# Field-embedding transposes of four tiles in one visit, and a ring of six gathered tiles

## The chip, the cores and the metric

The kernel runs on one core of one Trainium2 chip. The metric is the device time of one execution in microseconds (us); shorter is better. A time given "beside the span" is that of the execution that was profiled; the span runs from the first to the last profiled instruction.

## The reference

The computation is a recommendation tower over 2048 samples. Each sample has 40 id fields, and each id looks up a row of 64 floats in its field's table. All 780 pairs of fields are combined bilinearly, and the pair values go with 16 dense values through a small network:

```python
e = jnp.stack([tbl_0[ids[:, 0]], ..., tbl_39[ids[:, 39]]], axis=1)   # 2048 x 40 x 64
viW = jnp.einsum('bpd,pde->bpe', e[:, i_idx, :], W)                  # 780 pairs i < j, W[p] is 64 x 64
z = jnp.einsum('bpe,bpe->bp', viW, e[:, j_idx, :])                   # 2048 x 780
h = jnp.concatenate([z, dense_ctx], axis=1)
h = jnp.maximum(h @ W_top1 + b_top1, 0.0)    # 796 -> 512
h = jnp.maximum(h @ W_top2 + b_top2, 0.0)    # 512 -> 256
y = h @ W_top3                               # 256 -> 1
```

Everything is float32.

## The kernel before

The 2048 samples are worked in four chunks of 512. Chunk 0 is worked in two halves (called parts, `q` = 0 and 1) of 256 samples. Two neighbouring fields make a tile of 128 columns, so there are 20 tiles.

Per chunk there are N = 196 steps, 784 in all; in this text a step's number counts through all chunks (chunk 1 starts at 196, chunk 2 at 392, chunk 3 at 588). A step multiplies on TensorE (PE) into one of three buffers of `u` (two PSUM banks each), and VectorE (DVE) multiplies the buffer elementwise with the partner fields. There are two kinds. A column step (124 per chunk, PE line L1038, DVE line L952) keeps the samples in the free dimension; its product is summed over the 64 values by PE with a band of ones into `zacc` (L1052), two columns in one sum. A row step (72 per chunk, PE line L1024, DVE line L921) keeps the samples in the partitions; its product is summed by ScalarE (ACT, L838, 16 activations per row step), by DVE (L962) or by GpSimd (POOL, L755). `make_reducers` chooses who.

The fields have to arrive first. POOL issues indirect DMAs (L734), each of 128 rows of 64 floats; a tile of a whole chunk takes eight of them. Tiles 0 to 3 go to `first_fields`, the others to `gathered`, a ring of GRING tiles. Each issue waits for a step of DVE's progress (`issue_step`, from CHUNK_STEPS: first step and steps per field) and, for a ring slot, until PE has transposed what was in it. Two tiles (t, t+1) make one transpose, written (chunk, i, part) below, with t = 2i: PE transposes 128x128 blocks into one `u` buffer (L996), eight for a whole chunk and four for a half, and ACT copies the buffer to `emb` (L799), after two further copies for `emb_swap` (L797) where i = 2.

All engines follow one list, `ORDER`. Before a step come the transposes that are due at it (TRANSPOSE_STEPS, in the order chunk, part, i). At some transposes of the next chunk a group of the top network (`top`, L1084, L1090, L1096, L1103) of the chunk before is put behind them (TOP_STEPS), and twice per chunk the finished row sums are turned (`turn`, L1070, copied by ACT at L817 and L821). The function `make_room` moves ACT's row sums: one that stands less than HOLD = 2 pair steps ahead of a transpose is held back and written behind it. The `u` buffers go round in the order of their uses (pairs, transposes, turns, tops), so a use needs the third use before it to be done: multiplied, or copied by ACT.

I call a stretch of PE's order that holds only transposes, turns and tops a visit. Its instructions use the array in tiles of 128 rows, where the pair and sum steps use tiles of 64 rows by 32 columns.

Of the kernel before, what the change touches and what calls it, by code (L numbers as in the profile page):

```python
# [36 lines left out]
PRING = 6  # L37
LAG = 4
UBUF = 3
GRING = 4  # L40

SLOT = 4
WRING = 7
# [13 lines left out]
TOP_GROUPS = M1 // 2 + M2 // 2 + 1  # L57


TOP_FIRST = 18  # L60
TOP_EVERY = 19
# [7 lines left out]

FIRST_PART = 40  # L70
FIRST_STEPS = 2
CHUNK_STEPS = {1: (115, 3.9), 2: (280, 4.9), 3: (480, 4.9)}

POOL_FROM = 275

# [138 lines left out]
N = len(WHOLE)  # L214
# [21 lines left out]
def parts(c):  # L236
    return range(PARTS) if c == 0 else range(1)
# [8 lines left out]
def blocks_of(c, q):  # L246

    count = SUB // len(parts(c))
    return range(q * count, (q + 1) * count)
# [141 lines left out]
def make_needs():  # L391

    needs = {}
    for c in range(CHUNKS):
        for n, s in enumerate(STEPS[c]):
            for t in tiles_used(s):
                needs.setdefault((c, part_of(c, n), t // 2), n)
    return needs


NEEDS = make_needs()
# [19 lines left out]
def emb_before(c, i):  # L421

    x = c * TSTEPS + i - EMB_RING
    return EMB_LAST[divmod(x, TSTEPS)] if x >= 0 else None
# [7 lines left out]
def issue_step(c, q, f, s):  # L432

    if c == 0 and q == 0:
        return 0
    f += blocks_of(c, q).index(s) / len(blocks_of(c, q))
    i, j = int(f // 4), f % 4
    here = NEEDS[c, q, i]
    before = NEEDS[c, q, i - 1] if i else here - 4
    in_time = c * N + before + j * (here - before) / 4 - 14  # L440
    begin, every = CHUNK_STEPS[c] if c else (FIRST_PART, FIRST_STEPS)
    steady = begin + every * f
    return max(1, int(min(in_time, steady)))
# [7 lines left out]
def make_transpose_steps():  # L451

    out = []
    for c, i, q in TRANSPOSES:
        need = c * N + NEEDS[c, q, i]
        if c == 0 and q == 0:
            at = max(need - TRANSPOSE_LEAD, 0)
        else:
            issued = issue_step(c, q, 4 * i + 3, blocks_of(c, q)[-1])
            at = min(need - TRANSPOSE_LEAD, issued + LANDING[c])  # L460
            if emb_before(c, i) is not None:
                at = max(at, emb_before(c, i) + 2)
            assert issued <= at <= need
        out.append((at, c, i, q))
    return out


TRANSPOSE_STEPS = make_transpose_steps()


def make_top_steps():

    out = []
    for c in range(1, CHUNKS):
        at = [x for x, *_ in TRANSPOSE_STEPS if c * N + TOP_FIRST <= x < (c + 1) * N - TOP_EVERY][:TOP_GROUPS]
        while len(at) < TOP_GROUPS:
            at.append(at[-1] + TOP_EVERY)
        out += at
    return out


TOP_STEPS = make_top_steps()


# [16 lines left out]
def make_gathers():  # L501
# [3 lines left out]
    for c in range(CHUNKS):  # L505
        for q in parts(c):
            for t in range(T):
                place = ("first", t)
                if t >= FT:
                    rings[c, q, t] = len(rings)  # L510
                    place = ("ring", rings[c, q, t] % GRING)
                filled[place] = filled.get(place, 0) + 2 * len(blocks_of(c, q))
# [97 lines left out]
def pair_tower(nc, ids, tables, w_pairs, w_rows, dense, w1, b1, w2, b2, w3, y):  # L610
# [6 lines left out]
    with ctx:  # L617
        def sb(name, shape, dt=f32):
            return ctx.enter_context(nc.sbuf_tensor(name, shape, dt))

        def sem(name):
            return ctx.enter_context(nc.semaphore(name))
# [4 lines left out]
        first_fields = sb("first_fields", [P, 2, SUB, FF * DIM])  # L627
        gathered = sb("gathered", [P, GRING, SUB, P])
        emb = sb("emb", [P, 2 * EMB_RING, CB])
# [30 lines left out]
        first_gathered = [sem(f"first_gathered{t}") for t in range(FT)]  # L660
        rows_gathered = [sem(f"rows_gathered{i}") for i in range(GRING)]
        rows_transposed = sem("rows_transposed")
# [40 lines left out]
        def _(pool):  # L703
# [6 lines left out]
            def gather(c, q, t, e, s):  # L710
# [3 lines left out]
                if first and t < FT:  # L714
# [3 lines left out]
                    if c >= 2:  # L718
                        pool.wait_ge(rows_transposed, TURN_OF[c - 2, t // 2, len(parts(c - 2)) - 1] + 1)
                elif first and RING_USE[c, q, t] >= GRING:  # L720

                    at, part, tile = RING_ORDER[RING_USE[c, q, t] - GRING]
                    pool.wait_ge(rows_transposed, TURN_OF[at, tile // 2, part] + 1)
# [7 lines left out]
                else:  # L731
                    to = gathered[:, RING_USE[c, q, t] % GRING, s, e * DIM:(e + 1) * DIM]
                    done = rows_gathered[RING_USE[c, q, t] % GRING]
# [463 lines left out]
```

## Time and profile before

| | |
|---|---|
| time, median of 3 runs | 1158.18 us (1156.47 to 1160.94) |
| the profiled execution's own time | 1160.57 us |
| its span | 1158.8 us |
| PE busy | 1105.2 us (95%) |
| DVE busy | 947.9 us (82%) |
| ACT busy | 859.5 us (74%) |
| POOL busy | 744.8 us (64%) |
| TensorE's mean granted clock | 0.994 |

Busy is the union of an engine's instruction times. A matmul's end is modelled, so what PE lost at a place is better read from the starts of its instructions than from the idle time shown.

### The profile page before, as it was taken

What the parts mean: (1) busy time and instruction counts of PE and PEld (TensorE: products, weight loads), DVE (VectorE), ACT (ScalarE), POOL (GpSimd) and SP (SyncE); (2) the same over time, 40 slices, a digit from 0 to 9 for tenths busy, and PEclk for the clock granted to TensorE, in tenths of its full rate; (3) what the DMA queues carried; (4) which work ended last, traced back from release to release, by engine and by line L of the source; (5) the groups of instructions that cost most, each with busy time, mean ns of one, the idle gap of its engine ahead of it and who ended that gap; (6) DMA issues with size and microseconds to landing.
All of it is one profiled execution on the core that took longest, in us unless ns stands there. A gap on an engine that the chain in (4) does not pass through costs nothing.

```text
span 1158.8 us, 52361 instructions
## 1 busy us (share of the span) xinstructions
PE 1105.2 (95%) x21232; PEld 506.7 (44%) x21232; DVE 947.9 (82%) x830; ACT 859.5 (74%) x6607; POOL 744.8 (64%) x898
## 2 busy tenths in 40 slices
PE   2699989999999999999999999999999999999998
PEld 1356757665643333333363333333354333333333
DVE  0699878999859689999976689999984968999960
ACT  0677857999958569999965457898982845799971
POOL 7776777777756555778777567788777756522310
PEclk9999999999999999999999999999999999999999
DMA  6344444444423332232322232222222323211000
GB/s 187 83 121 131 125 121 121 130 139 130 103 52 87 86 88 72 76 86 76 77 63 78 71 93 76 76 78 77 77 68 49 94 73 93 70 58 58 19 3 18
DMA packets 60594, 98.02 MB, mean 85 GB/s; under 512 B 17072, under 2 KB 17088, under 8 KB 60352
## 3 DMA queue, kind: packets, MB, share of 16 engines
q1 hardware_dynamic: 35568, 64.57, 18.1%
q0 software_dynamic: 20480, 21.01, 9.3%
q10 hardware_dynamic: 4304, 9.09, 2.4%
q8 instruction: 167, 2.74, 1.0%
q14 instruction: 75, 0.61, 0.2%
HBM read 94.60 MB, written 0.01 MB: 82 GB/s over the span
## 4 chain that ended last, share of the span: by engine, by line
PE 76%; ACT 9%; POOL 5%; issue 5%; DVE 4%; DMA 1%; DVEq 0%; POOLq 0%
PE u L1038 30%; PE u L1024 18%; PE zacc L1052 15%; ACT row_prod L838 8%; PE u L1084 7%; PE u L996 3%; POOL gathered L734 3%; DVE prod L952 2%; PE u L1096 2%; POOL first_fields L734 1%; DVE row_prod L921 1%; POOL row_prod_p L755 1%; DMA gathered<-tbl,index 1%; PE u L1090 1%; PE u L1070 0%
## 5 line engine op out<-in xcount | busy, mean ns | idle before, releaser
L838 ACT ACTIVATE row_prod<-row_prod 128x64 f32<-128x64 f32 x3248 | 776.5, 242 | 65.9 <-DVE row_prod L921 65.7
L952 DVE TENSOR_TENSOR prod<-u,emb 128x1024 f32<-128x1024 f32 x496 | 588.8, 1217 | 102.0 <-PE u L1038 100.4
L734 POOL DMA_INDIRECT gathered<-tbl,index x512 | 484.7, 947 | 221.9 <-issue 121.5
L838 ACT ACTIVATION_READ_ACCUMULATOR row_prod<-row_prod 128x1 f32 x3248 | 613.1, 189 | 0.0
L1038 PE MATMUL u<-emb,weights 64*32 64x512 f32 (+1 forms) x9760 | 523.1, 507 | 3.5 <-DVE prod L952 2.1
L1024 PE MATMUL u<-row_weights,emb 64*32 64x512 f32 (+5 forms) x5632 | 337.7, 522 | 7.1 <-ACT emb L799 2.3
L1038 PEld LDWEIGHTS u<-emb,weights 64*32 64x32 f32 x9760 | 200.9, 107 | 235.7 <-issue 114.4
L921 DVE TENSOR_TENSOR row_prod<-u,first_fields 128x1024 f32<-128x1024 f32 x203 | 246.9, 1216 | 62.1 <-PE u L1024 61.8
L1052 PE MATMUL zacc<-prod,band 64*32 64x512 f32 (+1 forms) x4960 | 277.1, 504 | 0.7 <-DVE prod L952 0.5
L755 POOL TENSOR_TENSOR row_prod_p<-row_prod_p 128x512 f32<-128x512 f32 (+4 forms) x210 | 128.8, 614 | 90.8 <-DVE row_prod_p L921 77.1
L1024 PEld LDWEIGHTS u<-row_weights,emb 64*32 64x32 f32 x5632 | 118.4, 109 | 147.4 <-issue 56.7
L1052 PEld LDWEIGHTS zacc<-prod,band 64*32 64x32 f32 x4960 | 106.4, 107 | 115.4 <-issue 104.0
L734 POOL DMA_INDIRECT first_fields<-tbl,index x128 | 121.4, 948 | 49.9 <-issue 26.5
L799 ACT ACTIVATE emb<-u 128x1024 f32<-128x1024 f32 (+1 forms) x50 | 42.4, 849 | 86.5 <-PE u L996 86.3
L1084 PE MATMUL u<-z,w12s 128*128 128x512 f32 x192 | 85.6, 603 | 0.0
L853 ACT ACTIVATE h<-u,b1s 128x512 f32<-128x512 f32 x16 | 10.1, 684 | 80.6 <-PE u L1090 80.6
L1084 PEld LDWEIGHTS u<-z,w12s 128*128 128x128 f32 x192 | 36.4, 193 | 44.1 <-issue 43.7
L921 DVE TENSOR_TENSOR row_prod_p<-u,first_fields 128x1024 f32<-128x1024 f32 x42 | 51.1, 1217 | 4.5 <-PE u L1024 4.4
L921 DVE TENSOR_TENSOR row_prod_v<-u,first_fields 128x1024 f32<-128x1024 f32 x43 | 52.3, 1217 | 2.8 <-PE u L1024 2.6
L962 DVE TENSOR_REDUCE row_sums<-row_prod_v 128x16 f32<-128x1024 f32 x43 | 51.0, 1209 | 0.0
L996 PE MATMUL u<-ident,gathered 128*128 128x128 f32 x256 | 38.4, 284 | 13.2 <-DMA gathered<-tbl,index 12.8
L996 PEld LDWEIGHTS u<-ident,gathered 128*128 128x128 f32 x256 | 27.4, 142 | 40.7 <-DMA gathered<-tbl,index 14.4
(29 smaller groups left out, 151.9 us busy)
## 6 DMA issues: line engine op xcount, KB each, us to landing
weights<-w_pairs SPq DMA_DIRECT2D x155, 256.0 KB
row_weights<-w_rows SPq DMA_DIRECT2D x90, 256.0 KB
gathered<-tbl,index POOLq DMA_INDIRECT x512
w12s<-w_top ACTq DMA_DIRECT2D x8, 832.0 KB
first_fields<-tbl,index POOLq DMA_INDIRECT x128
w12s<-w_top ACTq DMA_DIRECT2D x4, 512.0 KB
index<-ids SPq DMA_DIRECT2D x1, 280.0 KB, 11.8
row_sums<-dense ACTq DMA_DIRECT2D x4, 32.0 KB
```

The lines of the kernel that those rows point to most:

```text
L734: pool.indirect_dma_start(out=to, out_offset=None, in_=tables[2 * t + e], in_offset=bass.IndirectOffsetOnAxis(ap=index[:, col:col + 1].bit ...
L755: nc.gpsimd.tensor_tensor(to, x[:, :, 0:width], x[:, :, width:2 * width], ALU.add).then_inc(rows_reduced_p if last else halved, 1)
L799: nc.scalar.activation(emb[:, first:first + 2, at], u[:, BUFFER[o], :, at], ACT.Copy).then_inc(emb_ready, 1)
L838: last = nc.scalar.activation(x, x, ACT.Copy, accum_out=row_sums[:, c % 2, s, q:q + 1])
L921: nc.vector.tensor_tensor(result, products, x, ALU.mult).then_inc(prod_ready, 1)
L952: nc.vector.tensor_tensor(result, products, x, ALU.mult).then_inc(prod_ready, 1)
L962: nc.vector.tensor_reduce(row_sums[:, c % 2, s, q:q + 2 * FF], x, mybir.AxisListType.X, ALU.add).then_inc(rows_reduced_v, 1)
L996: last = nc.tensor.transpose(u[:, b, h, s * P:(s + 1) * P], x, ident[:, :])
L1024: last = nc.tensor.matmul(u[g * TILE:(g + 1) * TILE, b, h, places], emb[half, emb_at(c, at // 2), samples_of], row_weights[half, x % PIECE ...
L1038: last = nc.tensor.matmul(u[of, b, h, to], weights[half, x % WRING, unit, of], y, start=True, stop=True)
L1052: last = nc.tensor.matmul(zacc[TILE * cg:TILE * cg + TILE, bank, samples(c, q)], band[half, TILE - 1 - r:2 * TILE - 1 - r], prod[half, (c ...
L1084: nc.tensor.matmul(u[:, b, m, :], w12s[:, x % 2, m * FULL + q, :], z_blocks(c, q)[:, 0, :], start=(q == 0), stop=False)
```

## The change

The list of transposes is post-processed. Where the transpose of an odd i (the second of four tiles) is due at a step not later than the step that first needs the one before it, the one before is put off to the same step. So two transposes stand directly behind each other, into two `u` buffers. TOP_STEPS takes each step once, so that four visits with tops are now up to four different paired steps; the reducers are chosen anew from them by the same rules. CHUNK_STEPS starts the gathers of chunks 1, 2 and 3 earlier by 10, 15 and 15 steps, and the ring has six slots. There are 52 visits before and 37 after.

```diff
-GRING = 4
+GRING = 6
...
-CHUNK_STEPS = {1: (115, 3.9), 2: (280, 4.9), 3: (480, 4.9)}
+CHUNK_STEPS = {1: (105, 3.9), 2: (265, 4.9), 3: (465, 4.9)}
...
         out.append((at, c, i, q))
+
+    for x in range(1, len(out)):
+        at, c, i, q = out[x]
+        if (c, q) != (0, 0) and i % 2 and at <= c * N + NEEDS[c, q, i - 1]:
+            out[x - 1] = (at,) + out[x - 1][1:]
     return out
...
-        at = [x for x, *_ in TRANSPOSE_STEPS if c * N + TOP_FIRST <= x < (c + 1) * N - TOP_EVERY][:TOP_GROUPS]
+        at = [x for x in sorted({x for x, *_ in TRANSPOSE_STEPS}) if c * N + TOP_FIRST <= x < (c + 1) * N - TOP_EVERY][:TOP_GROUPS]
```

The steps of the transposes and tops (a pair is in brackets; `top` marks a visit with a group of the top network):

```
before, part 1 of chunk 0:  75(with three others) 80 88 96 104 112 120 128
after:                      75(with two others) [80] [96] [112] [128]
before, chunk 1: 146 162 177 193 206 217top 240top 255top 271top 287
after:           [152] [183] 199 214top [245]top [277]top
before, chunk 2: 316 335 355 375 394 413top 433top 453top 473top 492
after:           [320]top [360] [399] [438]top [477]top
before, chunk 3: 516 535 555 575 594 609top 633top 653top 673top 692
after:           [520]top [560]top [599] 618top 638top [677]top, and a top alone at 696
```

The turns stay behind steps 205, 213, 397, 405, 593 and 601, and two at the end.

Three places in ACT's and PE's order follow. The first is ACT in part 1 of chunk 0. `emb<-u 128x2x256` is the copy of one transpose, `row_prod,row_sums<-row_prod 128x64 x16` the sum of one row step. Before, the copies of (0,3,1), (0,4,1) and (0,5,1) up to the chunk's first z copy, with eight pair steps between one transpose and the next on PE:

```order
L799 ACTIVATE emb<-u 128x2x256
L838 ACTIVATE row_prod,row_sums<-row_prod 128x64 x16
L799 ACTIVATE emb<-u 128x2x256
L838 ACTIVATE row_prod,row_sums<-row_prod 128x64 x32
L799 ACTIVATE emb<-u 128x2x256
L838 ACTIVATE row_prod,row_sums<-row_prod 128x64 x16
L805 ACTIVATE z<-zacc 128x2x256
```

After, from the copies of (0,2,1) and (0,3,1) to the same z copy:

```order
L804 ACTIVATE emb<-u 128x2x256 x2
L843 ACTIVATE row_prod,row_sums<-row_prod 128x64 x48
L804 ACTIVATE emb<-u 128x2x256
L843 ACTIVATE row_prod,row_sums<-row_prod 128x64 x16
L804 ACTIVATE emb<-u 128x2x256
L810 ACTIVATE z<-zacc 128x2x256
```

The two single copies are (0,4,1) and (0,5,1). On PE these two now stand directly behind each other (the next fence), and on ACT the sum of row step 91, which was held back, stands between their copies. The same pattern stands at (0,6,1) and (0,7,1) with row step 107.

PE at step 96 after the change, where one row of eight transposes is both of them:

```order
L1029 MATMUL u<-row_weights,emb 32x512 x8
L1001 MATMUL u<-ident,gathered 128x128 x8
L1043 MATMUL u<-emb,weights 32x256 x16
L1057 MATMUL zacc<-prod,band 32x256 x16
L1043 MATMUL u<-emb,weights 32x256 x32
```

Before, each of the two had a row of four of its own (`L996 MATMUL u<-ident,gathered 128x128 x4`), eight steps apart.

The second place is ACT around the end of chunk 0 and the start of chunk 1, up to the copy of the first turn (L817 before, L822 after). Before, from the copy of the transpose (1,2,0), with its two copies for `emb_swap`, on:

```order
L797 ACTIVATE emb_swap<-u 64x512 x2
L799 ACTIVATE emb<-u 128x1024
L838 ACTIVATE row_prod,row_sums<-row_prod 128x64 x80
L799 ACTIVATE emb<-u 128x1024
L838 ACTIVATE row_prod,row_sums<-row_prod 128x64 x32
L805 ACTIVATE z<-zacc 128x2x256
L838 ACTIVATE row_prod,row_sums<-row_prod 128x64 x48
L817 ACTIVATE z<-u 128x1024
L799 ACTIVATE emb<-u 128x1024
```

After:

```order
L802 ACTIVATE emb_swap<-u 64x512 x2
L804 ACTIVATE emb<-u 128x1024 x2
L843 ACTIVATE row_prod,row_sums<-row_prod 128x64 x64
L804 ACTIVATE emb<-u 128x1024
L843 ACTIVATE row_prod,row_sums<-row_prod 128x64 x16
L810 ACTIVATE z<-zacc 128x2x256
L843 ACTIVATE row_prod,row_sums<-row_prod 128x64 x48
L822 ACTIVATE z<-u 128x1024
```

The copy of (1,4,0) stood behind the turn's copy, and PE had made it at step 206. Now it stands four row sums and a z copy ahead of the turn's copy, at step 199, and those four sums come behind it.

The third place is ACT at the start of chunk 2, around the turn of chunk 1 (behind step 397). Before:

```order
L799 ACTIVATE emb<-u 128x1024
L805 ACTIVATE z<-zacc 128x1024
L838 ACTIVATE row_prod,row_sums<-row_prod 128x64 x16
L817 ACTIVATE z<-u 128x1024
L838 ACTIVATE row_prod,row_sums<-row_prod 128x64 x32
L821 ACTIVATE z<-u 64x512 x2
```

After:

```order
L810 ACTIVATE z<-zacc 128x1024
L822 ACTIVATE z<-u 128x1024
L804 ACTIVATE emb<-u 128x1024
L843 ACTIVATE row_prod,row_sums<-row_prod 128x64 x16
L804 ACTIVATE emb<-u 128x1024
L843 ACTIVATE row_prod,row_sums<-row_prod 128x64 x32
L826 ACTIVATE z<-u 64x512 x2
```

The transposes (2,4,0) and (2,5,0) now follow each other on PE at step 399, and again a held row sum (step 395) stands between their two copies. The same stands at step 599 for (3,4,0) and (3,5,0). At the other paired visits the two copies are neighbours.

## Rows read from the trace of the kernel before

**Rows 1.** The page: busy us, share of the span and instructions of each engine.

```profile
PE 1105.2 (95%) x21232; PEld 506.7 (44%) x21232; DVE 947.9 (82%) x830; ACT 859.5 (74%) x6607; POOL 744.8 (64%) x898
```

**Rows 2.** PE's timeline at (2,2,0): start us, length, engine, line, operation, names, shapes, count.

```profile
528.97 1.06 PE L1052 MATMUL zacc<-prod,band 64*32 64x512 f32 x16
529.83 1.06 PE L1024 MATMUL u<-row_weights,emb 64*32 64x512 f32 x16
530.83 1.09 PE L996 MATMUL u<-ident,gathered 128*128 128x128 f32 x8
531.85 1.09 PE L1038 MATMUL u<-emb,weights 64*32 64x512 f32 x16
```

**Rows 3.** PE's timeline at (2,5,0), which a top group follows.

```profile
608.22 1.09 PE L996 MATMUL u<-ident,gathered 128*128 128x128 f32 x8
609.15 2.31 PE L1084 MATMUL u<-z,w12s 128*128 128x512 f32 x5
```

**Rows 4.** PE's timeline at (0,3,1) and POOL's at its last gather (in brackets: idle before, releaser).

```profile
145.46 0.44 PE L996 MATMUL u<-ident,gathered 128*128 128x128 f32 x2
149.26 0.44 PE L996 MATMUL u<-ident,gathered 128*128 128x128 f32 x2 [3.37 <-DMA gathered<-tbl,index]
...
146.74 0.95 POOL L734 DMA_INDIRECT gathered<-tbl,index  x1 [0.31 <-DVE prod L952]
```

**Rows 5.** POOL's waits from 0 to 147 us: us in total, times, longest.

```profile
POOL gathered L734 <- PE u L996: 5.8, 3, 3.2
```

**Rows 6.** Busy times by stretch (PE, PEld, DVE, ACT, POOL), granted clock, DMA share, GB/s.

```profile
321.27:324.68 3.41, 3.41 (x56) 1.89 (x64) 0.42 (x1) 3.41 (x24) 2.50 (x4) 0.50 0.11 20
764.00:768.00 4.00, 2.47 (x48) 0.66 (x40) 2.02 (x3) 4.00 (x28) 3.37 (x4) 1.00 0.14 32
```

**Rows 7.** ACT: groups by line from 300 to 320 us, and timeline at two transposes.

```profile
L838 ACT ACTIVATE row_prod<-row_prod 128x64 f32<-128x64 f32 x80 | 19.1, 246 | 0.0
...
171.03 0.60 ACT L799 ACTIVATE emb<-u 128x512 f32<-128x512 f32 x1 [1.13 <-PE u L996]
...
277.75 1.20 ACT L797 ACTIVATE emb_swap<-u 64x512 f32<-64x512 f32 x2 [2.11 <-PE u L996]
278.95 1.02 ACT L799 ACTIVATE emb<-u 128x1024 f32<-128x1024 f32 x1
```

**Rows 8.** Timelines at steps 118 and 152: DVE, POOL (two gathers), PE.

```profile
204.07 1.21 DVE L921 TENSOR_TENSOR row_prod<-u,first_fields 128x1024 f32<-128x1024 f32 x1
...
206.80 0.94 POOL L734 DMA_INDIRECT gathered<-tbl,index  x1 [0.30 <-issue]
...
246.85 0.95 POOL L734 DMA_INDIRECT first_fields<-tbl,index  x1 [0.30 <-issue]
...
245.66 1.10 PE L1038 MATMUL u<-emb,weights 64*32 64x256 f32 x32
```

**Rows 9.** PE's timeline at steps 199, 206 and 207, and ACT's at the turn.

```profile
305.51 1.41 PE L1024 MATMUL u<-row_weights,emb 64*32 64x256 f32 x44
...
317.97 1.09 PE L1038 MATMUL u<-emb,weights 64*32 64x512 f32 x16
321.19 1.94 PE L1024 MATMUL u<-row_weights,emb 64*32 64x320 f32 x28 [2.13 <-ACT z L817]
...
320.13 1.01 ACT L817 ACTIVATE z<-u 128x1024 f32<-128x1024 f32 x1
```

**Rows 10.** PE's other waits of over 0.6 us in chunks 1 to 3, from its timeline.

```profile
586.68 1.07 PE L1070 MATMUL u<-ident,row_sums 128*128 128x128 f32 x8 [0.79 <-POOL row_sums L755]
...
766.35 1.09 PE L1024 MATMUL u<-row_weights,emb 64*32 64x512 f32 x16 [1.53 <-ACT emb L799]
...
857.74 1.07 PE L1070 MATMUL u<-ident,row_sums 128*128 128x128 f32 x8 [0.64 <-POOL row_sums L755]
...
883.13 0.66 PE L996 MATMUL u<-ident,gathered 128*128 128x128 f32 x4 [2.32 <-DMA gathered<-tbl,index]
```

**Rows 11.** DVE's timeline: the multiplication of the step that PE starts at 531.85.

```profile
533.04 1.23 DVE L952 TENSOR_TENSOR prod<-u,emb 128x1024 f32<-128x1024 f32 x1 [0.58 <-PE u L1038]
```

## The prediction

> **What bounds the kernel now.** I read the page's busy times first: PE works 95% of the span [rows 1]. The two timelines at ordinary visits say what a PE step costs: a pair or sum step starts 0.86 us after the one before it (528.97 to 529.83, [rows 2]). Laid against the order, step by step, PE keeps this pace nearly everywhere behind the start-up. So time is won where PE waits or changes its work, and lost where a new wait reaches PE. Three other queues matter because PE meets them at its visits. POOL issues a gather every 1.25 us (0.95 and 0.30 idle, [rows 8]) and is behind its due steps through all of chunk 0. ACT sums a row step in 3.83 us (19.1 us for five, [rows 7]) and holds `u` buffers until it has copied them. The clock is the third: behind a PE wait of 2.13 us the granted clock was 0.50, behind one of 1.53 us it was 1.00 [rows 6, 9, 10]. It lasted the 3.41 us of that row, so it costs 1.7 us; the clock is then at 1.2 instead of 2.4 GHz. I call this a slow stretch. Behind 3.37 and 2.32 us of waiting [rows 4, 10] there was one too.
>
> **A visit.** The step ahead of (2,2,0) takes 1.00 instead of 0.86 us, and the visit 1.02 us [rows 2]. A transpose that is followed by other work of 128 rows takes 0.93 us (608.22 to 609.15, [rows 3]). Two visits made one save 0.14 at the entry and 0.09 at the exit, about 0.24 us. There are 15 fewer visits: 5 before step 208, 1.2 us, and 10 after it, 2.4 us. The Trainium skill, TensorEngine Tiling (Array Packing), Key Properties, says that a change of tiling mode drains TensorE, and TensorE: Matmul & The Clock Gate, Single matmul latency, puts a drain at about 0.175 us. By that page, with a drain saved at either side, the 15 would give 5.3 us instead of the 3.6 us by the rows; the trace shows less at the exit.
>
> **Up to step 152.** The wait ahead of (0,3,1) goes. POOL waited three times for a ring slot, 5.8 us [rows 5]; six slots take all three away, and less the 0.3 us that stands between issues anyway POOL is 4.9 us earlier. The last gather of (0,3,1) went out at 146.74 and PE went on at 149.26 [rows 4], so a landing takes 2.5 us: now 144.3. PE, which makes (0,2,1) just ahead, comes there at 145.3. The gain is 3.7 us (3.37 shown; starts give about 0.3 more, as 317.97 to 321.19 less a step is 2.36 where 2.13 is shown, [rows 9]) and a slow stretch, 1.7. The merged visits up to step 118 give 0.5.
>
> Against it stand the held row sums at steps 96 and 112. With (0,4,1) starting at T, ACT copies it by T + 1.3 (0.6 us a copy), sums row step 91 until T + 5.2 and has (0,5,1) copied at T + 5.8 [rows 7]. PE spends 0.44 us on each transpose and 0.15 on the exit, then c96, a sum, c97, and at T + 3.6 wants the buffer of (0,5,1): a wait of 2.2 us. The same at step 112. 4.4 us together; 2.2 lies just over the shortest wait that had a slow stretch, so I count half of them, 1.7. Bounds are 0 and 3.4. Balance at step 118: -3.7 -1.7 -0.5 +4.4 +1.7 = +0.2 us.
>
> Next is the pair [152]. CHUNK_STEPS begins 10 steps earlier, but POOL was never idle there, so this moves nothing. Before, its last gather of part 1 went out at 206.80, 1.5 us behind its due step 118 (end 205.28), and the last of (1,1,0) at 246.85, 40.05 us later [rows 8]. With 4.9 us in hand POOL now waits for the due step: 205.6 + 0.2, then 40.05, then 2.5 to land: 248.3. PE would come to (1,1,0) at 245.66 + 0.2 - 1.0 (the old visit at 146 gone) + 1.0 = 245.9. It waits 2.4 us, with a slow stretch. Step 152 starts at 249.3 instead of 245.66. This is the step where the visit is too early for POOL: (1,1,0) used to be made at 162.
>
> From 152 to 183 PE needs 36.5 us (before 38.9 with two visits), plus the slow stretch, 1.7. At [183] it makes 0.9 + 0.9 + 0.2 and waits about 0.6, since ACT's copies of (1,2,0) take 1.2 + 1.0 [rows 7] where a single visit has a step more of room. Then 19.8 to step 199 and 1.0 for (1,4,0): step 199 starts at 310.8 (before 305.51, with one transpose less made).
>
> **The turn behind 205.** Before, ACT came to the turn's copy at 320.13, and PE, which wanted that buffer at 318.83, lost 2.36 us and a slow stretch [rows 9]. Now ACT stands idle for (1,4,0) ahead of step 199, copies it by 1.1 us behind the start of 199, and then has four row sums (15.3), a z copy (0.6) and the turn's copy (1.0): PE gets the buffer at 199 + 18.1. It wants it at 199 + 12.5 - 1.2 + 0.9 + 0.95 = 13.1 (305.51 to 317.97, less the transpose, two steps more). It waits 5.0 us instead of 2.4. Step 208 starts at 328.9 instead of 323.7, and it has the slow stretch still ahead, of which before only 0.5 was left: +6.4 us. All the gains up to here are in this number; two waits in turn, POOL's and ACT's, have eaten them.
>
> **The rest.** Ten visits fewer, -2.4. POOL's lead removes waits of before: its row sums ahead of the turns (0.79 and 0.64), the gather of (3,5,0), 2.32 with a slow stretch, which is now made at 599 with its gathers begun 15 steps earlier, and a copy that ACT was late with, 1.53, whose visit now has a top group near it [rows 10]. With 0.3 each, that is -6.5, and -1.7 for the clock. At steps 399 and 599 a held row sum stands between two copies of 1.0 us: the second is done at T + 7.1, and PE wants it at T + 4.1 (two transposes 1.9, two steps 2.2). 3.0 us each, and three in four with a slow stretch: 6.0 + 2.6. At [360] and [560] the `emb_swap` copies cost 0.6 each, 1.2. Where a gather is checked against the earlier due steps, POOL has 3 us or more in hand at every pair from step 214 on. Sum: +6.4 - 2.4 - 8.2 + 8.6 + 1.2 = **+5.6 us**, on the profiled execution's 1160.57 us. That execution lies 2.4 us above the median of the runs, 1158.18. On the median it is 1163.8; since all four of the half-counted terms lean on the clock I round down, to **1163 us**.
>
> The gather's landing is also priced by the Trainium skill: DMA: Bandwidth & Descriptors, Anatomy of one DMA, gives about 2.0 us and bytes by 436 GB/s. For 32 KB that is an estimate of 2.1 us instead of the 2.5 of the row, and by it the wait at 152 and the sum would be 0.4 us shorter.
>
> **The rivals.** (a) DVE is the one who makes it slower. Two transposes take two of the three buffers, so the next pair step needs the product of the step just before the visit. PE comes there 2.95 us after it started that step (0.86 + 0.14 + 0.93 + 1.02); DVE is done 2.42 us after (531.85 to 534.27, [rows 2, 11]). That leaves 0.5 us, and as soon as DVE is one multiplication (1.13 us between two) behind, PE waits 0.6 at each of 13 such visits of chunks 1 to 3: 7.8 us more, 1171. For it: DVE also sums two rows ahead of each top. Against it: at 531.85 DVE had been idle 0.58 us. It decides when DVE is over half a microsecond late.
> (b) The held sums cost nothing, as when PE's next steps come late for another reason, or ACT had time. Then the 4.4, 6.0 and slow stretches of 1.7 and 2.6 are off; POOL is queue-bound and (1,1,0) lands at 244.4, so step 152 comes 4.1 us earlier than above. -5.6 there and -8.6 later, plus what 152 keeps: about -7.5 in all, 1151, faster.
> (c) Only the visits count, the other waits neither go nor come: -3.6, 1154.6.
>
> **How the numbers follow.** The sum as worked out 0.52, with a range of its own of 1158.5 to 1168 (slow stretches none or all, -4.3 to +2.5, and 1 us of waiting at either gate); (a) 0.13; (b) 0.13; (c) 0.12; something else 0.10. A measurement of this kernel tells about 0.5%, 5.8 us, from no change: the bounds are 1152.4 and 1164. The sum's case lies half on either side of 1164, a little more below (0.28 and 0.24). Faster: most of (b) and a little of the unknown, 0.14. Slower: 0.24, (a) and 0.04, 0.41. Same: 0.45. The range to hold it 8 times in 10 goes from (b) near to (a): 1153 to 1171.
>
> **What would show it.** Right: a PE wait on ACT `emb` of about 2 us near 174 and 191 us, and of about 3 us at steps 399 and 599 (some 590 and 870 us); PE waiting for the gathers of `first_fields` near 246 us; 5 us for ACT z near 324 us; no wait near 146, 587, 765, 858 and 881 us; POOL without waits for PE; five or six stretches of clock 0.50. Wrong if ACT copies both buffers of a pair in one go at 96, 112, 399 and 599, if (1,1,0) has landed when PE comes, or if PE waits for DVE behind the pairs.

## The result

Six executions of the changed kernel took 1167.63 us in the median (1163.63 to 1171.18), six of the kernel before beside them 1158.15 us (1156.15 to 1160.94). The ratio is 1.0081, with a 95% interval of 1.0064 to 1.0097: a small loss. A second set, told below, gave 1.0071 (1.0047 to 1.0096). The forecast was 1163 us.

The profiled execution took 1165.26 us (span 1163.3), 4.7 us more than the profiled one of before. The page's first rows stand almost as they did [rows 1]:

```profile
PE 1101.5 (95%) x21232; PEld 521.9 (45%) x21232; DVE 946.5 (81%) x830; ACT 863.7 (74%) x6639; POOL 739.4 (64%) x892
```

What PE waited for is told by the view of waits: us in total, times, longest. The four largest of PE's rows after the change:

```profile
PE u L1001 <- DMA first_fields<-tbl,index: 24.1, 5, 12.7
PE u L1043 <- ACT emb L804: 7.8, 5, 2.5
PE u L1001 <- DMA gathered<-tbl,index: 6.8, 4, 2.9
PE u L1043 <- ACT z L822: 3.6, 1, 3.6
```

In the kernel before, the gathers into the ring were waited for 12.8 us, the copies to `emb` 2.3 us and the turn's copy 2.1 us. After the change a smaller row (L1029) adds 2.2 us to the 7.8 us for `emb`. So the ring of six and the earlier gathers did what they should (12.8 to 6.8), and ACT took it back (4.4 to 13.6). The rows on DVE rose too, from 6.0 to 8.1 us in all. The places, in PE's timeline, are the pairs at steps 96 and 112:

```profile
167.92 1.10 PE L1043 MATMUL u<-emb,weights 64*32 64x256 f32 x32 [0.47 <-DVE row_prod_v L926]
171.84 1.10 PE L1043 MATMUL u<-emb,weights 64*32 64x256 f32 x32 [1.05 <-ACT emb L804]
...
198.07 0.67 PE L1043 MATMUL u<-emb,weights 64*32 64x256 f32 x16 [1.37 <-ACT emb L804]
```

the pairs at 152 and 183, the turn behind 205, and the pairs at 399 and 599:

```profile
245.25 1.53 PE L1001 MATMUL u<-ident,first_fields 128*128 128x128 f32 x12
248.58 0.66 PE L1001 MATMUL u<-ident,first_fields 128*128 128x128 f32 x4 [1.79 <-DMA first_fields<-tbl,index]
...
290.07 1.09 PE L1029 MATMUL u<-row_weights,emb 64*32 64x512 f32 x16 [0.55 <-DVE prod L957]
...
328.92 3.13 PE L1043 MATMUL u<-emb,weights 64*32 64x512 f32 x29 [3.62 <-ACT z L822]
...
600.38 1.09 PE L1043 MATMUL u<-emb,weights 64*32 64x512 f32 x16 [2.44 <-ACT emb L804]
...
877.02 1.09 PE L1043 MATMUL u<-emb,weights 64*32 64x512 f32 x16 [2.51 <-ACT emb L804]
```

ACT's timeline at step 96 shows the held row sum between the two copies: the buffer of (0,5,1) is copied 4.3 us behind that of (0,4,1).

```profile
166.89 0.60 ACT L804 ACTIVATE emb<-u 128x512 f32<-128x512 f32 x1 [5.33 <-PE u L1001]
...
171.20 0.58 ACT L804 ACTIVATE emb<-u 128x512 f32<-128x512 f32 x1
```

The waits that the prediction wanted gone are gone: none at 146, 587, 765, 858 and 881 us. The starts of PE's steps can be subtracted where both kernels have the same transposes and top groups behind them. At 152, 402 and 608 the changed kernel has one transpose more behind it, about 1 us (us, each less before):

```
step                         84     118     152     208     211     402     608     705
changed kernel             -5.40   +0.16   +3.51   +5.21   +6.69   +8.56   +8.92   +4.36
changed kernel, second run -5.04   -0.27   +3.14   +4.48   +5.96   +7.96   +9.45   +4.89
sums held together         -3.84   -2.06   +2.56   +3.35   +5.73   +4.60  +12.32   +7.76
```

At 208 the trace of the kernel before has the instructions of steps 207 and 208 mixed; counted from the first of them, each value there is 0.9 us higher. The early gain of 5.4 us has gone by step 118. Between 151 and 152 the changed kernel falls back by 4.0 us, of which 2.0 are the pair of transposes and the rest is the wait for the gathers. The third row is an experiment, below.

### The profile page after: what moved, and what is told of

The parts are those of the page before. It is cut to its first block, busy times and chain, and to the rows that moved or that the text cites. A ratio compares the mean times of both kernels' runs of the same rounds, so it can differ in the third digit from the quotient of the medians.

```text
span 1163.3 us, 52387 instructions
## 1 busy us (share of the span) xinstructions
PE 1101.5 (95%) x21232; PEld 521.9 (45%) x21232; DVE 946.5 (81%) x830; ACT 863.7 (74%) x6639; POOL 739.4 (64%) x892
## 3 DMA queue, kind: packets, MB, share of 16 engines
q1 hardware_dynamic: 35568, 64.57, 18.1%
## 4 chain that ended last, share of the span: by engine, by line
PE 80%; DVE 7%; issue 6%; ACT 4%; POOL 3%; DMA 0%; DVEq 0%
PE u L1043 32%; PE u L1029 19%; PE zacc L1057 16%; PE u L1089 7%; DVE prod L957 4%; ACT row_prod L843 3%; PE u L1101 2%; PE u L1001 2%; DVE row_prod L926 2%; POOL first_fields L739 1%; POOL gathered L739 1%; ACT emb L804 1%; PE u L1095 1%; DVE row_sums L967 1%; DVE row_prod_v L926 1%
## 5 line engine op out<-in xcount | busy, mean ns | idle before, releaser
L957 DVE TENSOR_TENSOR prod<-u,emb 128x1024 f32<-128x1024 f32 x496 | 586.9, 1214 | 92.9 <-PE u L1043 92.4
L1043 PE MATMUL u<-emb,weights 64*32 64x512 f32 (+1 forms) x9760 | 530.1, 506 | 15.6 <-ACT emb L804 7.8
L1029 PE MATMUL u<-row_weights,emb 64*32 64x512 f32 (+5 forms) x5632 | 344.5, 519 | 7.5 <-ACT emb L804 2.2
L1043 PEld LDWEIGHTS u<-emb,weights 64*32 64x32 f32 x9760 | 209.4, 106 | 244.8 <-issue 96.0
L926 DVE TENSOR_TENSOR row_prod<-u,first_fields 128x1024 f32<-128x1024 f32 x204 | 247.6, 1214 | 76.7 <-PE u L1029 74.0
L1057 PE MATMUL zacc<-prod,band 64*32 64x512 f32 (+1 forms) x4960 | 285.4, 505 | 2.1 <-issue 1.6
L760 POOL TENSOR_TENSOR row_prod_p<-row_prod_p 128x512 f32<-128x512 f32 (+4 forms) x205 | 125.3, 611 | 110.1 <-DVE row_prod_p L926 96.7
L1029 PEld LDWEIGHTS u<-row_weights,emb 64*32 64x32 f32 x5632 | 124.2, 108 | 146.9 <-issue 48.8
L1057 PEld LDWEIGHTS zacc<-prod,band 64*32 64x32 f32 x4960 | 112.0, 107 | 113.9 <-issue 97.2
L926 DVE TENSOR_TENSOR row_prod_v<-u,first_fields 128x1024 f32<-128x1024 f32 x43 | 52.2, 1214 | 4.8 <-PE u L1029 4.6
L1001 PE MATMUL u<-ident,gathered 128*128 128x128 f32 x256 | 35.1, 281 | 7.2 <-DMA gathered<-tbl,index 6.8
```

The lines of the kernel that those rows point to most:

```text
L760: nc.gpsimd.tensor_tensor(to, x[:, :, 0:width], x[:, :, width:2 * width], ALU.add).then_inc(rows_reduced_p if last else halved, 1)
L926: nc.vector.tensor_tensor(result, products, x, ALU.mult).then_inc(prod_ready, 1)
L957: nc.vector.tensor_tensor(result, products, x, ALU.mult).then_inc(prod_ready, 1)
L1001: last = nc.tensor.transpose(u[:, b, h, s * P:(s + 1) * P], x, ident[:, :])
L1029: last = nc.tensor.matmul(u[g * TILE:(g + 1) * TILE, b, h, places], emb[half, emb_at(c, at // 2), samples_of], row_weights[half, x % PIECE ...
L1043: last = nc.tensor.matmul(u[of, b, h, to], weights[half, x % WRING, unit, of], y, start=True, stop=True)
```

## Experiments

Runs of this kernel fell on chips of two kinds. On one kind the kernel before takes 1158 to 1160 us, as above; on four other chips it took 1627 to 1650 us, because many of PE's steps take longer there (last section). A ratio below is always against the kernel before on the same chip, and the first number says which kind it was. A difference between kernels counts as told apart only on one chip.

**The row sums behind both transposes.** One line of `make_room`: a held row sum is written behind the last transpose of a visit, not behind the first.

```diff
-        if o[0] in ("transpose", "top", "copy z") and (i + 1 == len(order) or order[i + 1][0] != "top"):
+        if o[0] in ("transpose", "top", "copy z") and (i + 1 == len(order) or order[i + 1][0] not in ("top", "transpose")):
```

> The changed kernel with one edit: a held row sum is no longer written between two neighbouring transposes, but behind both (steps 96, 112, 399, 599). If the held sums cost what the changed trace shows (PE loses 2.9 us at step 399 and 3.3 us at step 599 against the kernel before, and 1.3 and 1.6 us at 96 and 112, with slow stretches in part of the executions), the time falls by 6 us for the two late places and by up to 4 us for the two early ones, as far as the wait for gathers at step 152 does not eat it: 1157 to 1161 us. If they cost nothing, because PE would have waited there for something else (DVE, with two of three buffers taken), it stays at 1165 to 1168. PE then shows a wait for DVE behind these pairs in place of the wait for ACT emb.

> The kernel held_together once more, because the chip of the first four runs took 1650 us for the kernel before, where its PE steps were stretched by issue gaps. If this execution is again near 1158 us for the kernel before, the expectations are those of held_together: 1157 to 1161 us if the held row sums cost what the changed trace shows (2.9 and 3.3 us at steps 399 and 599, 1.3 and 1.6 us at 96 and 112, the early two in part eaten by the wait for gathers at step 152), 1165 to 1168 us if they cost nothing.

On a chip where the kernel before took 1160.0 us it took 1168.87 us (1164.52 to 1170.87), ratio 1.0073 (1.0058 to 1.0089). The expected 1157 to 1161 us did not come, and nothing was gained on the changed kernel, which took 1166.15 us on the same chip (last experiment); the two are not told apart. Its first run was on a chip of the other kind (1650 us before), 1.0054 (1.0032 to 1.0077). The trace of the one at 1169 us says why. The waits for ACT behind the pairs of 96, 112, 399 and 599 are gone, with none for DVE in their place at 399 and 599; both copies now run in one go, and PE is at step 118 2.2 us earlier than in the changed kernel. PE's timeline then, at the pair of 152, at the turn behind 205, and at the second turns of chunks 1 and 2:

```profile
247.17 1.12 PE L1001 MATMUL u<-ident,first_fields 128*128 128x128 f32 x4 [3.04 <-DMA first_fields<-tbl,index]
...
327.06 3.67 PE L1043 MATMUL u<-emb,weights 64*32 64x512 f32 x32 [3.62 <-ACT z L822]
...
608.18 1.45 PE L1029 MATMUL u<-row_weights,emb 64*32 64x320 f32 x24 [1.92 <-ACT z L826]
...
882.21 1.29 PE L1029 MATMUL u<-row_weights,emb 64*32 64x320 f32 x8 [2.68 <-ACT z L826]
```

PE came to (1,1,0) 2.7 us earlier and waited 1.25 us longer: the visit at 152 is bound by POOL, which issues its last gather there at 246.10 us in the changed kernel and at 244.65 us here, each time 2.5 us before PE goes on. Of the 2.2 us won by step 118, 0.95 are left at step 152. The sums that were taken out of the pairs at 399 and 599 are still ahead of the turn's copy (L826), six and two steps later. PE, no longer held up at the pair, comes to the turn before ACT. From 590 to 610 us ACT is busy for 17.3 of the 20 us, and from 600 on without a gap: its row sums, in two instructions each, fill the time, and only transposes (2.5 us) were waited for at length:

```profile
L843 ACT ACTIVATE row_prod<-row_prod 128x64 f32<-128x64 f32 x56 | 13.4, 242 | 0.0
L843 ACT ACTIVATION_READ_ACCUMULATOR row_prod<-row_prod 128x1 f32 x56 | 10.5, 188 | 0.0
L804 ACT ACTIVATE emb<-u 128x1024 f32<-128x1024 f32 x2 | 1.9, 1022 | 2.5 <-PE u L1001 2.5
```

So a wait of 2.44 us at 399 became one of 1.92 us at 405 with a slow stretch, and 2.51 us at 599 became 2.68 us with two.

**Pairs kept, chunk 1's gathers back at 115.** `CHUNK_STEPS` with `1: (115, 3.9)` as before. The pair (1,0,0), (1,1,0) is then made at 162 instead of 152, (1,4,0) at 206 instead of 199, and the choice of who sums the rows shifts with the visits. With it a held row sum stands between the two copies at four of the later pairs, at steps 320 and 360 as well as at 399 and 599. Without and with the sums held together, on one chip (1628.8 us before):

> The changed kernel with the one number of chunk 1 put back from (105, 3.9) to (115, 3.9): the ring of six, the pairs and the earlier gathers of chunks 2 and 3 stay. Theory (the loss lies at step 152 and the turn behind step 205, both children of that number, and in the held row sums): the wait for the gathers of tile (1,1,0), 1.8 us in the changed kernel's trace with 3.5 us more by step 152, goes; the turn behind 205 waits 2.4 us as before and not 3.6; the held sums at steps 96, 112 and 399, 599 still cost 1 to 3 us each. Ratio to the kernel before 1.003, 1162 us (1.001 to 1.005). Rival (the cost comes with the pairs themselves, wherever they stand): the ratio stays at the changed kernel's 1.008, 1168 us.

> The same, and the row sums held behind the second transpose of a pair, not between the two copies. Theory: with step 152 and the held sums between copies both gone, what is left is two or three fewer waits and 15 fewer visits at 0.24 us against one wait for the pair (0,2,1), (0,3,1): ratio 1.000, 1159 us (0.998 to 1.002), below the kernel with chunk 1 alone put back by 1 to 4 us. Rival 1 (ScalarE is only late one place further on, as at 606 and 880 us in the kernel that held the sums together): the two are within 1 us of each other. Rival 2 (pairs cost by themselves): 1.007.

1641.77 us, ratio 1.0076 (1.0052 to 1.0101), and 1631.04 us, ratio 1.0006 (0.9991 to 1.0021). The first ratio is the one that its rival had named (1.008, pairs cost by themselves, wherever they stand). The second kernel has the same pairs at the same steps and does not lose, so it is not the pairs. This is the clearest of the comparisons: the two differ in the one line of `make_room`, and by 0.7% or 10.7 us. PE's waits, of the first and of the second:

```profile
PE u L1029 <- ACT emb L804: 7.4, 3, 4.0
PE u L1043 <- ACT emb L804: 5.9, 4, 2.4
```

```profile
PE u L1029 <- ACT emb L804: 1.1, 1, 1.1
```

The longest wait of the first is behind the pair at 360, where the changed kernel waits 0.43 us; others are 2.22 us behind the pair at 320, 2.44 at 399 and 2.40 at 599:

```profile
855.49 1.96 PE L1029 MATMUL u<-row_weights,emb 64*32 64x512 f32 x16 [4.00 <-ACT emb L804]
```

The second kernel has one more such row, 0.8 us at L1043. 13.3 us of waiting for ACT's copies became 1.9, and nearly all of it stayed won. But 6.2 of the 13.3 us lie at 320 and 360, so the 10.7 us are not what the held sums cost the changed kernel. Here ACT is not late at the next turn. By the kernels' order, row steps 400 and 596 are summed by POOL in this version, where the kernel with chunk 1 at 105 has them on ACT, just ahead of the second turns. No kernel moves these two sums alone, so that they are the reason is argued and not shown. The version with 105 waits at the second turn of chunk 2 and the one with 115 doesn't, on the chip where both ran:

> The kernel held_together with CHUNK_STEPS of chunk 1 back at (115, 3.9): its pairs are at steps 162 and 193 (instead of 152 and 183), (1,4,0) is back behind the turn at 206 (instead of ahead of it at 199). If step 152 comes too early for POOL and the copy of (1,4,0) ahead of the turn makes ACT late, the waits at 246 us (2.1 us) and most of that at 325 us (4.4 us against 2.4 before, with a slow stretch in both) go: 4 to 6 us less than held_together. If instead POOL's queue is what decides wherever the pair stands, the wait only moves to step 162 and the time is that of held_together within 2 us.

1654.1 us, 1.0034 (1.0016 to 1.0051), against 1660.48 us, 1.0054, for the sums held together with 105. The difference cannot be put down to step 152: on these chips the two also differ by some 15 us between steps 120 and 127 (last section). The latter's trace has this row, and the former's none for L826 among its waits:

```profile
PE u L1029 <- ACT z L826: 2.1, 1, 2.1
```

The same kernel as the second of these, on a third chip of the second kind:

> The kernel held_chunk1 (chunk 1's gathers back at 115, row sums behind both transposes) once more, for a chip on which the kernel before takes about 1159 us. Against the kernel that holds the sums behind both transposes and keeps 105, which took 1168.9 us, a ratio of 1.0073: by the theory the wait of 3.05 us at step 152 with its stretch at half the clock (1.7 us), the turn's 3.6 us for 2.4 with one such stretch more, and the waits of 1.9 and 2.7 us for the turns' copies at 606 and 880 us go, 8 to 10 us in all, but the waits of the kernel before for the gathers of its pair-less tiles partly come back. Ratio 1.000, 1160 us (0.998 to 1.003). Rival (pairs or earlier gathers cost by themselves): 1.005 to 1.008.

1628.66 us against 1628.49, ratio 1.0006 (0.9988 to 1.0023).

**The ring and the gathers without pairs.** The kernel before with `GRING = 6` alone, and with the three new chunk starts as well:

> The kernel before with a ring of six slots and nothing else. By my sum POOL gains 4.9 us, the wait ahead of (0,3,1) goes (3.37 us shown, 3.7 by starts) and with it a slow stretch of 1.7 us, so chunk 0 ends 5 us earlier; the later waits stay or shrink. Since ACT is late at the turn behind 205 anyway, part may be lost there: 2 to 6 us less than before, 1152 to 1156 us. If a ring slot was never what PE waited for, 1158.

> The kernel before with a ring of six and the earlier CHUNK_STEPS, but no pairing: transposes of chunks 1 to 3 follow their gathers, so (1,1,0) is at step 152 and (1,3,0) at 183 here too, and (1,4,0) ahead of the turn. If those early steps are what costs, chunk 1 loses against ring_only (a wait for gathers at 152, a longer one for ACT at the turn, 3 to 5 us), and chunks 2 and 3 win the 6 to 8 us of POOL waits at their starts: 1150 to 1157 us. If it is the pairing as such that costs, this kernel is the fastest of the four by 3 us or more.

> The kernel before with the ring of six and all three new chunk starts, but no pairs: (1,1,0) is transposed at step 152, where the pair stands in the changed kernel, and (1,0,0) alone at 136. Theory (the wait at 152 belongs to the gathers, not to the pair): PE waits 1.5 to 3 us for the gathers of (1,1,0) there, and the ratio is 1.003, 1162 us (1.001 to 1.005). Rival (the wait comes from the pair, since both tiles are wanted at once): no wait over 0.6 us at step 152, and the ratio is 0.997 to 1.000, 1155 to 1158 us.

The ring alone: 1644.13 us, 0.9964 (0.9946 to 0.9982), the only kernel of the study that is clearly below the one before, as expected in direction (0.2 to 0.5%). With the chunk starts: 1651.96 us, 1.0022 (1.0006 to 1.0038) on the same chip, and 1627.65 us, 0.9993 (0.9975 to 1.0011) on another. On the first chip the earlier gathers cost 7.8 us, more than the ring had gained; on the second the ring alone did not run, and the two together are not told apart from the kernel before. PE is slower on these chips and POOL is not late, so the wait at 152, for which these were made, was not to be seen, and they decide nothing about it. They do show something about the second turns. Neither has a pair. Both have row steps 594 and 596 on ACT between the transpose at step 599 and the second turn of chunk 2, as the kernel with the sums held together has them. Both wait for ACT's copy of that turn, 2.0 and 2.2 us. This is the row of the second:

```profile
PE u L1024 <- ACT z L821: 2.2, 1, 2.2
```

So this wait needs no pair; ACT's two sums ahead of the turn are enough. The changed kernel shows no such wait, but there PE is held up by 2.51 us at the pair just ahead.

**Two row sums to DVE.** `on_vector.update((196, 202))` in `make_reducers`, on top of the sums held together and chunk 1 at 115, so that ACT is free for the turn behind 205:

> As the second kernel of this set, and the row sums of steps 196 and 202 go from ScalarE (16 pairs of instructions, 3.9 us each) to VectorE (one reduction, 1.21 us each). Theory: the turn behind step 205 finds ScalarE free, its wait of 2.4 us before and 3.6 us after goes to under 1 us, and the half-clock stretch behind it (1.7 us) with it: 3 to 4 us under the second kernel, ratio 0.997, 1155 us (0.995 to 0.999), so below both the kernel before and the changed one. Rival (VectorE is itself late there, or ScalarE is late at the next copy): within 1 us of the second kernel.

> Chunk 1's gathers back at 115, the row sums behind both transposes of a pair, and the row sums of steps 196 and 202 on VectorE, once more, for a chip on which the kernel before takes about 1159 us. By the theory its trace is free of the five waits that the changed kernel added: none of 1.5 us or more behind the pairs of steps 96 and 112, at step 152, at the turn behind 205 (3.6 us in the changed kernel, 2.1 before), or at 399 and 599; ratio 0.996 to 1.000, 1155 to 1159 us. Rival 1 (pairs and earlier gathers cost by themselves, wherever they stand): 1.005 to 1.008. Rival 2 (the waits go but half-clock stretches come all the same): waits under 10 us in all behind step 80, and yet 1.003 or more with a mean clock under 0.990.

1629.89 us, ratio 0.9996 (0.9980 to 1.0013), beside 1.0006 for the same without it: no difference that is told apart. A second time, on another chip: 1630.61 us, 1.0013 (0.9995 to 1.0032). With or without the edit PE doesn't wait there at the turn behind 205. On the first of these chips no idle stretch of PE over 1.2 us is left between step 199 and the last top groups, on the second one of 1.71 and one of 1.82 us, at other places. So the edit had nothing to remove. Whether it wins where the turn is waited for 3.6 us stays open.

**The changed kernel again.**

> The changed kernel itself once more, to stand beside the variants on the chips they ran on. Where the kernel before takes about 1159 us: 1.008 again (1.006 to 1.010), the same four waits of 1.8 to 3.6 us. Where it takes 1625 to 1650 us: by the theory that what is lost is ScalarE's copies behind held row sums and the wait at step 152, the first is worth what the kernel with chunk 1 alone put back lost against the one that holds the sums together as well (0.7% there), the second what putting chunk 1 back gained (0.2%): ratio 1.009, 11 to 18 us (1.007 to 1.011), and ScalarE's copies are waited for 10 us or more in all. Rival (where PE has gaps of its own a late copy is hidden in them): 1.000 to 1.005.

It fell on a chip of the first kind: 1166.15 us (1162.35 to 1172.05) against 1159.39, ratio 1.0071 (1.0047 to 1.0096). Its trace has the same waits as the first to within 0.5 us (1.36 us at 152, 3.62, 2.44, 2.51).

## Why the prediction was right

The direction, the size and most places came out. Several terms were off and cancelled in part, so how close the sum came to the traced execution is in part luck. The time alone would not have decided it either: the median of 1167.63 us is nearer to the 1171 us of rival (a) than to the 1163 us forecast. What decides is the trace.

- **The visit.** The pair at step 360 has no wait ahead of PE's first step behind it:

```profile
542.26 1.06 PE L1057 MATMUL zacc<-prod,band 64*32 64x512 f32 x16
543.25 1.97 PE L1001 MATMUL u<-ident,gathered 128*128 128x128 f32 x16
545.15 1.09 PE L1043 MATMUL u<-emb,weights 64*32 64x512 f32 x16
```

By the starts it takes 1.00 and 1.89 us. Two single visits take 2.02 us each [rows 2], 4.04 in all, and this one with a step of 0.86 us more takes 3.75: 0.29 us saved, for 0.24 predicted.
- **The gain at step 80.** -3.7 and -1.7 gave -5.4, measured -5.40. But 0.3 us of that stood already at step 70, ahead of the first difference in PE's order.
- **The held sums at 96 and 112.** Right in place and cause, too large in size: 2.2 us each and 1.7 for the clock were put down, 1.3 and 1.6 us came by the starts (1.05 and 1.37 shown), without a slow stretch. ACT's second copy ended at 171.78, at T + 5.6 with T = 166.20 (5.8 predicted). It was PE that came later, at T + 4.3 instead of T + 3.6: with two buffers in transposes it first waited 0.47 us for DVE (its row at 167.92 us). The balance at 118 was right (+0.16 for +0.2) because further small losses, 0.58 us and less at a time, filled up what the held sums did not take.
- **The pair at 152.** A wait of 1.8 us shown (2.0 by the starts) for 2.4. PE came to (1,1,0) at 246.2 for 245.9 and made the first of its two tiles before it had to wait. POOL, which sets the end, was where it was put (last gather 246.10 for 245.85, landed 2.5 us later as before), so step 152 began at 249.16 for 249.3. No slow stretch came behind it here; behind the 3.04 us of the experiment one did. The 1.7 us counted for it were missing, and yet PE needed 37.9 us from step 152 to the pair at 183, where 38.2 had been put down with it. A wait of 0.55 us for ACT at step 153 is part of what filled it up; the rest stays open, and that it fits is luck.
- **Step 183.** 0.55 us for 0.6, but not for the cause given. ACT's two copies for `emb_swap` had ended at 289.38 us; PE waited for DVE, whose product of the step ahead of the visit ended at 290.02, behind a row sum that DVE had made just before.
- **Step 199 and the turn.** 311.07 for 310.8; 328.92 for 328.9. By the starts the wait is 4.4 us (3.62 shown) where 5.0 was counted: PE wanted the buffer 13.4 us behind the start of step 199 and not 13.1, and ACT had it ready after 17.9 us and not 18.1. At step 211 +6.7 for +6.4.
- **399 and 599.** By the starts 2.9 and 2.8 us for 3.0 each. The slow stretches, 2.6, came in neither place in the first trace and in one in the second. Without them the sum is +3.0 us, and the first trace measured +4.5. Of the 1.5 us between them 0.3 stood at step 211; by the rest the other terms behind it were too favourable.
- **The slow stretches in all.** Five or six were forecast; the first trace has one between start-up and end, the second two, with one more in the start-up.
- **Rival (a)**, DVE, was priced at 0.6 us at each of 13 visits of chunks 1 to 3. PE waited for DVE behind one of them, at 183 (0.55 us; 0.75 in the second trace), and behind the pairs at 96, 112 and 128 (0.47, 0.35 and 0.35 us). The mechanism exists, with 1.7 us in the first trace for the 7.8 us of its price. Since a wait for DVE behind the pairs was named as a sign of being wrong, this sign came in part.
- **Rival (b)**, that held sums cost nothing, fell by the waits at four places. But the converse, that their 7.4 us can be had back by moving them, fell too where ACT is nearly full: they went on to the next copy. They were had back in the version with chunk 1 at 115, where other row sums were on POOL. **Rival (c)**, visits alone and 1154.6 us, fell with the same waits.
- **The median.** The rounding down, from 1163.8 to 1163, had the wrong sign. On the medians the loss is 9.5 us in the first set and 6.8 in the second, while the spans of the traced executions are 4.5 and 5.0 us longer. The twelve executions spread over 10 us, those of before over 5. The profiled one had one slow stretch in its body, and the highest mean granted clock of its set (0.998; the others 0.985 to 0.996). Each stretch of 3.41 us at half the clock lowers the mean over 1160 us by 0.0015, so the others had 1 to 9 more; this is an estimate from the means. Before, the traced execution had three behind waits and one in the start-up, and was 2.4 us over its median. What I took from before, that waits of 2.13 us and more have a slow stretch behind them and one of 1.53 us has none, so that half or three in four of the waits near and over 2 us would have one, was the part that failed (last section).

That the visit at 152 and the turn cost what their rows show is read from three traces, not from a kernel that undoes them on a chip of the first kind; those made for it ran on the others. No kernel has the ring and the pairs with all three of the old chunk starts.

## What to carry to other kernels

When two copies follow each other behind a pair of transposes, see what the copying engine has between them, and then see what it has ahead of its next copy: on an engine without gaps a row sum that is moved was only waited for one place later; it was won where other sums had gone to another engine. A wait that is taken away ahead of a queue-bound gate (here POOL's gathers at 152) returned in large part at the gate; look at the gate first. And where a wait can trip the clock, give the time a spread, and don't take one traced execution for the median.

## What the hardware showed

**The half clock is not set by the length of the wait alone.** Windows of granted clock (us; busy times of PE, PEld, DVE, ACT, POOL; clock; DMA share; GB/s), in the changed kernel behind waits of 3.62, 2.44 and 2.51 us:

```profile
329.51:332.92 3.41, 3.41 (x48) 1.06 (x31) 2.00 (x2) 3.41 (x30) 2.53 (x3) 0.50 0.38 96
600.40:603.80 3.40, 3.40 (x76) 1.42 (x80) 1.73 (x2) 3.40 (x30) 3.20 (x4) 1.00 0.12 24
877.02:880.40 3.38, 3.38 (x68) 1.54 (x76) 1.23 (x1) 3.38 (x30) 2.77 (x3) 1.00 0.19 33
```

in its second run behind the same 2.51 us:

```profile
877.75:881.16 3.41, 3.41 (x37) 1.12 (x42) 1.14 (x1) 3.40 (x23) 3.06 (x3) 0.50 0.17 34
```

and with the sums held together behind 3.62 and 1.92 us:

```profile
325.48:332.30 6.82, 5.25 (x52) 1.42 (x56) 2.45 (x2) 6.82 (x52) 4.99 (x7) 0.50 0.29 67
608.78:612.19 3.41, 3.41 (x59) 2.17 (x59) 1.23 (x1) 3.41 (x30) 2.50 (x4) 0.50 0.11 25
```

So 1.92 us was enough once, 2.44 us was not twice, the same 2.51 us did and didn't, and 3.62 us gave one stretch or two. The double one began at 325.48 us, 1.6 us before PE went on at 327.06, so part of it fell into the wait. PE had 37 matmuls in the half-clock window at 877.75, which begins 1.3 us behind the wait, and 76 in the 3.41 us from the same place (878.31) in the first trace.

**Some chips slow PE's steps.** On four chips the kernel before took 1627 to 1650 us. DVE and ACT need the same time per instruction there (a product on DVE 1220 ns in the mean for 1214, a read of ACT's sum 188 for 189), but PE waits for "issue", which it hardly does elsewhere; with the sums held together and chunk 1 at 115:

```profile
PE u L1029 <- issue: 47.6, 61, 2.4
```

All its rows of this kind make 89 us, of some 460 us by which its span is longer than that of the changed kernel. The rest lies inside what is shown as busy: by the starts half of the steps keep to 0.88 us, but one in ten takes 2.4 us or more, where on the other chips nine in ten stay under 0.95. The kernel with ring and gathers, from its windows around steps 120 to 127:

```profile
320.00:335.00 15.00, 13.41 (x276) 7.25 (x274) 9.87 (x9) 8.41 (x66) 6.32 (x7) 1.00 0.30 83
335.00:350.00 15.00, 9.23 (x64) 2.30 (x65) 2.55 (x3) 8.90 (x65) 11.34 (x13) 0.70 0.21 48
350.00:365.00 15.00, 8.57 (x49) 2.45 (x53) 0.49 (x1) 0.00 (x0) 6.86 (x8) 0.51 0.09 18
365.00:380.00 15.00, 13.72 (x297) 7.81 (x289) 9.96 (x9) 7.07 (x56) 6.60 (x7) 1.00 0.31 86
```

For some 25 us PE started a matmul only every 0.7 us at times, where it starts 18 to 20 a us on either side; DVE and ACT had next to nothing to do from 350 us on, and the clock was at half from 341 to 365 us. The three executions traced there with chunk 1's gathers at 105 need 39 to 40 us from step 120 to 127, those with 115 need 22 to 25; part of the difference comes back by step 287. What starves PE there was not tried.
